# A GRU recurrence on one core: gate products in the order R, Z, N, the new state by one scan, the candidate's bias by a product in PSUM, four steps a loop turn

## The reference

```python
def cell(h, x):                       # h: [8, 512], x: [8, 512] of one position
    gi = x @ W_ih + b_ih              # all 256 positions can be done ahead
    gh = h @ W_hh + b_hh              # W_hh: [512, 1536], needs the state before
    i_r, i_z, i_n = jnp.split(gi, 3, axis=-1)
    h_r, h_z, h_n = jnp.split(gh, 3, axis=-1)
    r = jax.nn.sigmoid(i_r + h_r)
    z = jax.nn.sigmoid(i_z + h_z)
    n = jnp.tanh(i_n + r * h_n)       # h_n holds its part of b_hh
    h_new = (1.0 - z) * n + z * h
    return (h_new, h_new)
x = x + hs                            # hs: the 256 states
```

## Time and profile before

| what | value |
|---|---|
| time, median of 3 runs | 2892.21 us (2890.47 to 2893.78) |
| span of the profiled execution | 2889.4 us; its own time is not given apart from the span |
| recurrence in that span | 1661.4 to 2767.0 us, 1105.7 us, 256 steps |
| TensorE busy / DVE / ACT / POOL over the span | 73% / 42% / 34% / 18% |

### The profile page before, as it was taken

One profiled execution on the slowest core, in us unless ns is written; L12 is line 12 of the kernel. 1 busy time (PEld: TensorE's weight loads), 2 busy tenths in 40 slices (PEclk: granted clock), 3 DMA queues, 4 the chain that ended last, 5 costly groups with the idle time before them and its releaser, 6 DMA issues. The chain is left out here.

```text
span 2889.4 us, 91237 instructions
## 1 busy us (share of the span) xinstructions
PE 2099.3 (73%) x38252; PEld 1231.6 (43%) x38284; DVE 1209.9 (42%) x3495; ACT 968.4 (34%) x1884; POOL 521.1 (18%) x1184
## 2 busy tenths in 40 slices
PE   1556768787786868778669977777777777777754
PEld 0122223232332223233234466666666666666631
DVE  3425435443443535344300044444444444444456
ACT  1142434344352524335122233333333333333313
POOL 4012212022222202222100011111111111111102
PEclk8687889998898989899689999999999999999977
DMA  3352423435341443530220000000000000000001
GB/s 74 43 73 60 90 34 100 58 88 78 81 74 31 101 46 88 78 85 7 68 89 0 0 1 0 0 0 0 0 0 0 0 0 0 0 0 0 0 34 58
DMA packets 51980, 111.19 MB, mean 38 GB/s; under 512 B 11985, under 2 KB 38097, under 8 KB 46049
## 3 DMA queue, kind: packets, MB, share of 16 engines
q1 hardware_dynamic: 47328, 110.03, 19.5%
q0 software_dynamic: 4608, 0.60, 0.2%
HBM read 80.60 MB, written 29.41 MB: 38 GB/s over the span
## 5 line engine op out<-in xcount | busy, mean ns | idle before, releaser
L823 PE MATMUL gate<-whh,hT 128*8 128x128 f32 x24576 | 718.6, 273 | 134.5 <-POOL xT L721 93.9
L823 PEld LDWEIGHTS gate<-whh,hT 128*8 128x8 f32 x24576 | 644.8, 90 | 167.1 <-POOL xT L721 110.2
L394 DVE TENSOR_REDUCE mx<-MX 128x1 f32<-128x512 f32 x768 | 494.0, 686 | 474.2 <-PE MX L524 468.9
L459 ACT ACTIVATE pr<-ST 128x1024 f32<-128x1024 f32 x384 | 373.5, 1023 | 465.2 <-PE ST L547 239.1
L524 PE MATMUL MX<-K,Q 116*128 116x512 bf16 (+1 forms) x768 | 299.2, 427 | 192.6 <-DMA Q<-d_rows 102.4
L785 ACT ACTIVATE act<-pre 128x32 f32<-128x32 f32 x512 | 118.4, 231 | 727.8 <-DVE pre L744 466.8
L742 DVE STREAM_TRANSPOSE trn<-gate 128x128 f32<-128x128 f32 x256 | 81.2, 317 | 527.4 <-PE gate L823 527.4
L524 PEld LDWEIGHTS MX<-K,Q 116*128 116x128 bf16 (+1 forms) x768 | 69.0, 99 | 466.9 <-DVE mx L394 215.3
L814 PE MATMUL gate<-identz,giz 128*8 128x32 f32 x8192 | 109.8, 193 | 143.3 <-issue 142.2
L716 POOL TENSOR_TENSOR rbias<-act,bT 128x32 f32<-128x32 f32 x256 | 61.6, 241 | 723.1 <-ACT act L785 723.1
L544 PE MATMUL ST<-Q,K 119*128 119x512 bf16 x512 | 147.1, 413 | 49.4 <-DMA Q<-nmp 49.2
(11 more groups left out here) (141 smaller groups left out, 2193.3 us busy)
## 6 DMA issues: line engine op xcount, KB each, us to landing
Q<-d_q SPq DMA_DIRECT2D x112, 256.0 KB
K<-d_k SPq DMA_DIRECT2D x112, 256.0 KB
d_q<-piece_q SPq DMA_DIRECT2D x96, 128.0 KB
d_k<-piece_k SPq DMA_DIRECT2D x96, 128.0 KB
xin<-in_x_dram SPq DMA_DIRECT2D x8, 512.0 KB, 12.7
x<-in_x_dram SPq DMA_DIRECT2D x8, 512.0 KB, 12.5
out_dram<-sq SPq DMA_DIRECT2D x4, 1024.0 KB, 4.3
wih<-in_w_ih_dram SPq DMA_DIRECT2D x1, 3072.0 KB, 9.7
```

What stands on the lines that cost most here:

```text
L394: dve.reduce_max(mx[:, u, 4 * i + qb:4 * i + qb + 1], banks[0][:, :], AX.X).then_inc(mx_red[u].sem, 1)
L459: act.activation(pr[:, kc % 2, 2 * p:2 * p + 2, :], ST[:, 2 * p * T:(2 * p + 2) * T].rearrange("p (a t) -> p a t", a=2), ACT.Exp, scale=SC ...
L823: last = pe.matmul(ps[g][32 * j:32 * j + B, 0:P], hT[:, u, c, :], whh[:, c, o:o + P], start=c == 0 and g != Z, stop=c == C - 1)
```

## The change

Order of the products R, Z, N instead of R, N, Z. Z has two PSUM banks in turn (`psZ[q]`), and POOL, no longer ACT, copies `giz`. The candidate's hidden bias goes into N's bank by one product of a 64 by 128 selection matrix with a 64 by 128 array of bias rows, both float32r (`pick`, `bn_rows`: the rounded bias and what rounding left). POOL's two `rbias` instructions are gone. State, `by` and `plus` hold pairs; with by = (0, n) and plus = (1 - z, z h), a scan `s = by * s + plus` over 64 numbers leaves the new state in every second place. TensorE waits for `s_h` in every step. A turn has four steps. Three more loads and some vector instructions come ahead of the input products.

```diff
+        state = sb("state", [P, 2, C, B, 2])
+        by = sb("by", [P, C, B, 2])
+        plus = sb("plus", [P, C, B, 2])
+        psZ = pg[0:2]
+        def gi_at(i, u, g):
+            return giu[:, bass.ds(i + u // U, 1), u % U, g, :, :].rearrange("p i c b -> p (i c) b")
             # SyncE
+                sp.dma_start(pick_ld[:], pick_in).then_inc(s_ld, 16)
+                sp.wait_ge(s_init, 1)
+                for j in range(2):
+                    sp.dma_start(bn[32 * j:32 * j + C, :], bhn_rows).then_inc(s_ld, 16)
             # GpSimd
-                        pool.wait_ge(s_act[R], i * 2 + (u + 1))
-                        pool.tensor_tensor(rbias[:, u, 0], act[:, R], bias_n, ALU.mult).then_inc(s_rb, 1)
-                        pool.wait_ge(s_rb, i * 4 + (2 * u + 1))
-                        pool.tensor_tensor(rbias[:, u, 1], rbias[:, u, 0], gi2[...], ALU.add).then_inc(s_rb, 1)
+                        pool.wait_ge(s_psz, now)
+                        pool.tensor_copy(giz[:, q], gi_at(i, u + 2, Z)).then_inc(s_giz, 1)
+                        pool.wait_ge(s_h, i * U + (u + 2))
+                        pool.tensor_tensor(xt, xt, state[:, 1 - q, :, :, 1], ALU.add).then_inc(s_acc, 1)
             # VectorE, one step
+                        dve.wait_ge(s_ps[tR], now)
+                        dve.transpose(trn[:, R, :], psR[:, 0:P]).then_inc(s_tr[tR], 1)
+                        dve.wait_ge(s_tr[tR], t + (u + 2))
+                        dve.tensor_tensor(pre[:, 0], tr[R], gi_at(i, u, R), ALU.add).then_inc(s_pre[tR], 1)
+                        dve.wait_ge(s_psz, now)
+                        dve.transpose(trn[:, Z, :], psZ[q][:, 0:P]).then_inc(s_trz, 1)
+                        dve.wait_ge(s_z, now)
+                        dve.tensor_scalar(plus[:, :, :, 0], zg[:], -1.0, 1.0, ALU.mult, ALU.add).then_inc(s_chain, 1)
+                        dve.tensor_tensor(plus[:, :, :, 1], h0, zg[:], ALU.mult).then_inc(s_chain, 1)
+                        dve.wait_ge(s_ps[tN], now)
+                        dve.transpose(trn[:, N, :], psN[:, 0:P]).then_inc(s_tr[tN], 1)
+                        dve.wait_ge(s_tr[tN], t + (u + 2))
+                        dve.wait_ge(s_r, now)
+                        dve.tensor_tensor(tmp[:], tr[N], rg[:], ALU.mult).then_inc(s_chain, 1)
                         dve.wait_ge(s_chain, t * 3 + (3 * u + 3))
+                        dve.tensor_tensor(pre[:, 1], tmp[:], gi_at(i, u, N), ALU.add).then_inc(s_pre[tN], 1)
                         dve.wait_ge(s_acc, t + (u + 1))
+                        dve.wait_ge(s_n, now)
+                        dve.tensor_tensor_scan(pairs(state[:, 1 - q]), pairs(by[:]), pairs(plus[:]), 0.0, ALU.mult, ALU.add).then_inc(s_h, 1)
             # ScalarE, one step: sigmoid R, sigmoid Z (now before tanh), tanh N into by[:, :, :, 1]
             # TensorE, one step
+                        pe.wait_ge(s_giz, t + (u + 1))
+                        pe.wait_ge(s_trz, t + (u + 1))
...
+                        pe.wait_ge(s_tr[tR], t + (u + 1))
+                        pe.wait_ge(s_h, t + (u + 1))
+                        for c in range(C):
+                            last = products(psR, R, q, c, c == 0, c == C - 1)
+                        last.then_inc(s_ps[tR], 1)
+                        for c in range(C):
+                            last = products(psZ[q], Z, q, c, False, c == C - 1)
+                        last.then_inc(s_psz, 1)
+                        pe.wait_ge(s_tr[tN], t + (u + 1))
+                        pe.matmul(psN[:, 0:P], pick[:], bn_rows[:], start=True, stop=False)
+                        for c in range(C):
+                            last = products(psN, N, q, c, False, c == C - 1)
+                        last.then_inc(s_ps[tN], 1)
```

More of the change, by code:

```diff
@@ L675, in recurrent_and_last_layer @@
-        act = sb("act", [P, GATES, C, B])
-        tmp = sb("tmp", [P, 3, C, B])
-        ps = [pb(f"gate{g}", [P, 512]) for g in range(GATES)]
+        pre = sb("pre", [P, 2, C, B])
+        rg = sb("rg", [P, C, B])
+        tmp = sb("tmp", [P, C, B])
+        ps = [pb(f"gate{g}", [P, 512]) for g in range(3)]
         pg = [pb(f"pg{g}", [P, 512]) for g in range(4)]
-        (s_ld, s_init, s_chain, s_rb, s_gi_mm, s_gi_ev, s_h, s_acc, s_giz) = (
-            sem(n) for n in ("gru_loaded", "gates_cleared", "step_product", "bias_gated", "gi_products",
-                             "gi_ready", "state_ready", "state_added", "giz_ready"))
@@ L683, in recurrent_and_last_layer @@
[L683 to L686, removed]
-        R, Z, N = 0, 1, 2
-        NLD = 16 * 6
+        psZ = pg[0:2]
+        (s_ld, s_init, s_chain, s_gi_mm, s_gi_ev, s_acc, s_giz, s_r, s_n) = (
+            sem(n) for n in ("gru_loaded", "gates_cleared", "step_product", "gi_products",
+                             "gi_ready", "state_added", "giz_ready", "reset_ready", "candidate_ready"))
@@ L705, in _ @@
             @block.gpsimd
             def _(pool):
[L707 to L713, removed]
-                        pool.wait_ge(s_act[R], i * 2 + (u + 1))
-                        pool.tensor_tensor(rbias[:, u, 0], act[:, R], bias_n, ALU.mult).then_inc(s_rb, 1)
-                        pool.wait_ge(s_rb, i * 4 + (2 * u + 1))
[L718 to L721, removed]
+                pool.wait_ge(s_gi_ev, 4 * MT)
@@ new lines, in _ @@
+                for u in range(2):
+                    pool.tensor_copy(giz[:, u], gi4[:, u, Z]).then_inc(s_giz, 1)
+                with pool.Fori(0, T // U) as i:
+                    for u in range(U):
+                        q = u % 2
+                        now = i * U + (u + 1)
+                        pool.wait_ge(s_psz, now)
+                        pool.tensor_copy(giz[:, q], gi_at(i, u + 2, Z)).then_inc(s_giz, 1)
+                        pool.wait_ge(s_h, i * U + (u + 2))
+                        xt = xv[:, :, bass.ds(i, 1), u, :].rearrange("p c i b -> p c (i b)")
+                        pool.tensor_tensor(xt, xt, state[:, 1 - q, :, :, 1], ALU.add).then_inc(s_acc, 1)
@@ L723, in _ @@
             @block.vector
             def _(dve):
-                dve.memset(giT[:, T:T + 2, :], 0.0).then_inc(s_init, 1)
-                for g in range(3):
-                    dve.memset(ps[g][:, 0:P], 0.0).then_inc(s_init, 1)
+                dve.memset(bn[:], 0.0).then_inc(s_init, 1)
+                dve.memset(giT[:, T:T + U, :], 0.0).then_inc(s_init, 1)
+                dve.memset(psR[:, 0:P], 0.0).then_inc(s_init, 1)
+                dve.memset(by[:], 0.0).then_inc(s_init, 1)
+                dve.memset(state[:, 1], 0.0).then_inc(s_init, 1)
@@ L732, in _ @@
+                dve.tensor_copy(bn_rows[0:32], bn_hi[0:32].bitcast(fp32)).then_inc(s_init, 1)
+                dve.tensor_tensor(bn_rows[32:64], bn[32:64], bn_hi[32:64].bitcast(fp32), ALU.subtract).then_inc(s_init, 1)
+                dve.sem_inc(s_acc, 2)
+                for s in (*s_tr, s_h):
+                    dve.sem_inc(s, 1)
+                dve.sem_inc(s_trz, 2)
                 dve.wait_ge(s_gi_ev, 4 * MT)
-                with dve.Fori(0, T // 2) as i:
-                    for u in range(2):
-                        t = i * 2
+                with dve.Fori(0, T // U) as i:
+                    for u in range(U):
+                        q = u % 2
+                        t = i * U
@@ L736, in _ @@
                         now = t + (u + 1)
[L737 to L761, removed]
+                        h0 = state[:, q, :, :, 1]
@@ L776, in _ @@
                                      ACT.Identity, bias=bsum[:, m:m + 1]).then_inc(s_gi_ev, 1)
[L777 to L789, removed]
+                with a.Fori(0, T // U) as i:
+                    for u in range(U):
+                        now = i * U + (u + 1)
+                        a.wait_ge(s_pre[tR], now)
+                        a.activation(rg[:], pre[:, 0], ACT.Sigmoid).then_inc(s_r, 1)
+                        a.wait_ge(s_trz, i * U + (u + 3))
+                        a.activation(zg[:], tr[Z], ACT.Sigmoid).then_inc(s_z, 1)
+                        a.wait_ge(s_pre[tN], now)
+                        a.activation(by[:, :, :, 1], pre[:, 1], ACT.Tanh).then_inc(s_n, 1)
             @block.tensor
@@ L803, in _, with products @@
                         last.then_inc(s_gi_mm, 1)
[L804 to L810, removed]
+                pe.wait_ge(s_init, 12)
+                pe.wait_ge(s_gi_ev, 4 * MT)
+                def products(bank, g, q, c, first, done):
+                    for j in range(4):
+                        o = g * D + P * j
+                        last = pe.matmul(bank[32 * j:32 * j + B, 0:P], state[:, q, c, :, 1], whh[:, c, o:o + P], start=first, stop=done)
+                    return last
@@ L811, in _ @@
+                with pe.Fori(0, T // U) as i:
+                    for u in range(U):
+                        q = u % 2
+                        t = i * U
                         pe.wait_ge(s_giz, t + (u + 1))
```

(8 more changed lines are left out.)

48 lines of the change are left out of this document (34 added, 14 removed).

## The result

The changed kernel took 3049.11 us (median of 4, 3044.07 to 3052.54) against 2891.34 before (median of 4, a fourth execution added): ratio 1.0546, 95% interval 1.0529 to 1.0564. It is slower, as forecast, but by 158 us where the forecast was 88. That is above the 2925 to 3030 that had the chance of 0.70, and only 1 us inside the wider range, which ends at 3050. The profiled execution took 3044.07 with a span of 3042.2.

The account below looks back on a forecast made before the run. A dependent chain bounds the recurrence; +0.85 order, +0.30 bias product, -0.15 `rbias` stall, -0.43 scan, -0.225 POOL wait make +0.345 a step, +88 us over 256 steps, 2981 us; range 2925 to 3030 (0.70), wider 2905 to 3050.

Parts of the forecast that it names:

- the wider range: Whole program: 2905 to 3050 us, from a nearly free bias product to most of the drain, held about 0.8.
- What bounds: Recurrence: a chain with no full engine, 4.319 us a step before, 4.66 forecast after.
- The order, +0.85: N as third gate: its transpose waits for all products, 2.86 us instead of 2.01, in every step.
- The bias product, +0.30: Between Z's and N's products on the chain: its stream, losses at both changes and some load, 0.30 us a step.
- The drain rival: Bias product: TensorE waits out record tails on both sides and the load, 0.61 us, 3060 in all; chance 0.12.
- the free product: Bias product: no loss at a change, 0.05 us; part of the faster rival, chance 0.10.
- N's transpose to tanh, 0.91: Chain from N's transpose to tanh: 0.91 us, before 1.06, with no `rbias` stall and a 0.15 gap before `pre`.
- The scan, 0.28: Step's end on DVE: scan over 64 numbers takes 0.28 us, the middle between 0.234 and 0.32.
- The gaps around the scan, 0.03 and 0.05: Step's end: 0.03 us from tanh's end to the scan, 0.05 from the scan to the next products.
- The wait on POOL, -0.225: Step's start: TensorE always waits for `s_h`, saving 0.45 us in every second step, 0.225 a step.
- Four steps a turn, zero: Loop: branches hide in DVE's wait for R and TensorE's wait for the state, so no change.
- Ahead of the loop: Before the input products: three more small loads and POOL's first copies cost zero to 2 us, taken as 1.

Follow-up runs that it names:

- e1: Changed kernel with the bias product left out: 2949.37 us, ratio 1.0208 to the kernel before.
- e4: Changed kernel with the old gate order R, N, Z on all three engines: 2961.73 us, ratio 1.0252 to the kernel before.
- e9: Changed kernel with the bias product done as four float32 products in column groups, in its old place: 3009.37 us, ratio 1.0412 to the kernel before.
- e12: Changed kernel with N's input part copied by POOL to a fixed address two steps ahead: 3016.69 us, ratio 1.0438 to the kernel before.
- e3: Changed kernel with the two waits exchanged before the scan and before R's products, late one first: 3008.22 us, ratio 1.0406 to the kernel before.
- e5: Kernel before, with TensorE waiting for the state in both steps of a turn: 2834.44 us, ratio 0.9813 to the kernel before.
- e10: Changed kernel with two steps a loop turn instead of four: 3048.31 us, ratio 1.0545 to the kernel before.
- e8: Changed kernel with order R, N, Z, bias product before the state wait, late waits first, scan kept: 2847.44 us, ratio 0.9855 to the kernel before.
- e7: Like e8, but with the old three-instruction end instead of the scan: 2824.41 us, ratio 0.9764 to the kernel before.
- e11: e7 with a semaphore of its own for h - n, so no register arithmetic follows the wait for z: 2798.80 us, ratio 0.9682 to the kernel before.
- e2: Changed kernel with the bias product and its wait moved before R's products and the state wait: 2946.20 us, ratio 1.0197 to the kernel before.

## Why the prediction was right, and where its size was off

- **What bounds.** Right: a chain with no full engine, 4.93 a step by the timeline and 4.926 by the stretch, with the clock at 1.00 as before.
- **The order, +0.85.** Right: 2.86 without the bias product in e1, against 2.01. The 0.05 behind the last record does not follow from its working, though. 63 spacings of 0.0275 are 1.73, and with the 0.20 that 95 spacings leave of 2.81 gate N ends 0.08 before its transpose, which would give 2.89. That 2.86 came out was luck of 0.03. And +0.85 is what the order does to N's transpose, not what it would save to undo it: undoing it alone (e4) gives back 0.32, as Z's tail then ends the step.
- **The bias product, +0.30.** It measured 0.38. The losses in the attention rows were the right guide to 0.1. The drain rival (0.61) and the free product (0.05) both fell. The Trainium skill ("TensorEngine Tiling (Array Packing)", Key Properties) states that a change of tiling mode drains TensorE. The trace fits this in that something is lost at a change (0.13 ahead of the product; in e9, without a change, nothing), though loads that no longer run ahead would show the same. But neither side waits for a record to end: the product starts at 2005.70, while Z's last record ends at 2005.76, and N's loads start 0.25 behind the product's start, before its record of 0.32 has ended.
- **N's transpose to tanh, 0.91.** Measured 0.91 (2007.08 to 2007.99), with a gap of 0.14 for the 0.15; by e12 the loop-dependent address is its cause.
- **The scan, 0.28.** Measured 0.292. The Trainium skill ("DVE: opcode table, instruction layouts, handler registers and perf-mode slots", section Datapath and trigger behaviour) has the scan at half throughput. The estimate from that, 0.30 to 0.32, was about as near to the trace as the middle of the rows.
- **The gaps around the scan, 0.03 and 0.05. This is the term that was wrong.** They measured 0.10 and 0.15, 0.17 of the 0.27 that the step came out too long. I took them from places where the late wait was the only one. The changed kernel has two waits there with the late one second, and e3 shows that this alone is 0.16 of the 0.17. It could have been read before: L761 starts 0.10 behind Z's sigmoid (2006.09 to 2006.19), where L758 starts 0.03 behind tanh; both wait on ACT, and the source has two waits in front of the one and one in front of the other.
- **The wait on POOL, -0.225.** Right; e5 gives it alone as some 54 us, for the 57.6 of 0.45 in 128 steps.
- **Four steps a turn, zero.** Right by e10. **Ahead of the loop**: no loss seen; the first products start at 1658.94, before at 1661.37.
- **The range.** That it held 3049 was luck. Its upper end, 3050, was drawn for a dearer bias product, "most of the way into the drain", and what filled it was in the main the two gaps, for which the range had no room of its own. By the time alone the drain rival's 3060 was nearer than 2981; only the timeline and e1 tell them apart. Of the signs named ahead, N's transpose (3.25 for 3.1 to 3.2) and the products' start behind the scan (0.15 for 0.05) missed.

The miss adds up: 0.09 to N's transpose, 0.07, 0.01 and 0.10 around the scan, 0.27 a step, 69 us: 2981 + 69 = 3050.

## What to carry to other kernels

In a recurrence, first list what the last product feeds: put last the gate with the shortest way to the new state, and move every product that does not need the state in front of the wait for it. Of two waits in front of an instruction write the one that comes late first, and keep register arithmetic (loop-dependent addresses and counts) away from it. A fused instruction is worth its place only together with the instructions that it wants done before it: the scan won 0.12 over two plain ones and still lost to three that began earlier (e8 against e7). And compare a rewrite with the repaired original: of the 92 us that e11 gains on the kernel before, some 54 are what one changed wait gains by itself (e5).

## What the runs showed of the hardware that was not expected

Two waits written directly behind one another with the late one second cost 0.07 us more on DVE and 0.09 more on TensorE than with the late one first (e3). Register arithmetic between a late wait and its instruction costs 0.08 to 0.10 (e11, e12). A float32r product of 64 by 128 with 128 columns shows as one record of 0.32 with a load of 0.18. It costs 0.38 between column-group products, more than four float32 products in groups do (0.22, e9), and nothing that shows where TensorE idles (e2).
